# Other orders of the steps on each engine and other PSUM places in a pipelined decoder layer

## The reference

```python
x = _layernorm(x + linear_attention(x, Wq, bq, Wk, bk, Wv, bv, Wo, bo))
x = _layernorm(x + cross_attention(x, ctx, ctx))
x = _layernorm(x + ffn(x, w_gate, w_up, w_down))
```

## Time and profile before

| | |
|---|---|
| time, median of 3 runs | 1811.16 us (1810.85 to 1812.78) |
| the profiled execution | 1813.1 us |
| its span, first to last instruction | 1811.3 us |
| mean granted clock of TensorE | 0.964 of full speed |
| TensorE (PE) busy | 1626.2 us, 90% of the span |
| VectorE (DVE) busy | 1380.3 us, 76% |
| ScalarE (ACT) busy | 826.8 us, 46% |
| GpSimd (POOL) busy | 184.3 us, 10% |

### The profile page before, as it was taken

The page is one execution under the profiler, slowest core; times in us unless marked ns, Lnnn a source line. Parts: engine busy times, 40 slices in busy tenths (PEclk is TensorE's granted clock), DMA queues, the critical chain, the costliest instruction groups (busy, mean ns, idle before and its releaser), DMA issues.

```text
span 1811.3 us, 25396 instructions
## 1 busy us (share of the span) xinstructions
PE 1626.2 (90%) x10470; PEld 1002.6 (55%) x10470; DVE 1380.3 (76%) x1759; ACT 826.8 (46%) x784; POOL 184.3 (10%) x154
## 2 busy tenths in 40 slices
PE   7776599999999999999999999999999999996865
PEld 5443465656666555656656555656556655653533
DVE  3567887787968687787969697877869687876846
ACT  1124237264554536363554536363544536372633
POOL 0222301001010201011010202010010202010000
PEclk9887799999999999999999999999999999997979
DMA  5242220405050311304050401304050502204000
GB/s 204 50 111 97 48 18 30 51 7 74 1 80 1 67 13 39 41 18 63 1 79 1 75 6 50 30 25 56 2 79 1 79 1 57 24 19 47 7 7 12
DMA packets 100122, 75.73 MB, mean 42 GB/s; under 512 B 6044, under 2 KB 85148, under 8 KB 99496
## 3 DMA queue, kind: packets, MB, share of 16 engines
q1 hardware_dynamic: 100008, 74.10, 23.1%
HBM read 52.58 MB, written 20.97 MB: 41 GB/s over the span
## 4 chain that ended last, share of the span: by engine, by line
PE 78%; DVE 9%; ACT 8%; issue 2%; DMA 1%; POOL 1%; SPq 1%; POOLq 0%; ACTq 0%; DVEq 0%
PE psum L508 12%; PE psum L658 11%; PE psum L596 7%; PE psum L609 6%; PE psum L685 6%; PE psum L702 6%; PE psum L532 6%; PE psum L554 6%; PE psum L575 5%; ACT ffn_mem L733 3%; PE psum L638 2%; PE psum L694 2%; DVE ffn_mem L1086 2%; PE psum L677 1%; PE psum L542 1%
## 5 line engine op out<-in xcount | busy, mean ns | idle before, releaser
L733 ACT ACTIVATE ffn_mem<-psum 128x1024 f32<-128x1024 f32 x160 | 159.9, 1021 | 390.4 <-PE psum L630 148.7
L1013 DVE TENSOR_REDUCE mneg<-psum 128x4 f32<-128x1024 f32 x256 | 306.5, 1219 | 37.7 <-PE psum L575 34.4
L736 ACT ACTIVATE attn_mem<-psum 128x1024 f32<-128x1024 f32 x256 | 249.4, 1019 | 87.2 <-PE psum L609 85.0
L575 PE MATMUL psum<-kst,attn_mem 96*128 96x256 bf16 x1024 | 149.4, 277 | 25.2 <-DMA attn_mem<-q_dram 8.7
L609 PE MATMUL psum<-attn_mem,kst 98*128 98x512 bf16 x512 | 148.1, 391 | 21.2 <-ACT attn_mem L736 10.7
L1144 POOL TENSOR_TENSOR grstd<-gvare,neg_half 128x1 f32<-128x1 f32 x32 | 17.6, 551 | 1353.6 <-DVE gvare L912 1353.6
L1105 DVE TENSOR_TENSOR ffn_mem<-ffn_mem 128x1024 f32<-128x1024 f32 x128 | 150.8, 1219 | 1.2
L685 PE MATMUL psum<-had,ffn_mem 128*128 128x128 f32 x1024 | 127.2, 277 | 22.2 <-ACT ffn_mem L733 22.2
L596 PE MATMUL psum<-attn_mem,vpad 128*32 128x256 f32 x2048 | 138.1, 394 | 2.5 <-ACT attn_mem L736 2.5
L575 PEld LDWEIGHTS psum<-kst,attn_mem 96*128 96x128 bf16 x1024 | 96.1, 99 | 76.1 <-issue 20.7
L824 ACT ACTIVATE ffn_mem<-psum,sc 128x1024 f32<-128x1024 f32 x64 | 69.7, 1114 | 148.2 <-PE psum L658 148.0
(11 more groups left out here) (152 smaller groups left out, 2489.5 us busy)
## 6 DMA issues: line engine op xcount, KB each, us to landing
attn_mem<-q_dram SPq DMA_DIRECT2D x192, 128.0 KB, 7.7
q_dram<-work SPq DMA_DIRECT2D x48, 256.0 KB, 2.8
x_in<-in_x SPq DMA_DIRECT2D x16, 512.0 KB, 3.8
out<-r SPq DMA_DIRECT2D x32, 256.0 KB, 2.2
ffn_mem<-in_L_ffn_w_gate SPq DMA_DIRECT2D x1, 4096.0 KB, 21.6
ffn_mem<-in_L_ffn_w_up SPq DMA_DIRECT2D x1, 4096.0 KB, 16.0
ffn_mem<-in_L_ffn_w_down SPq DMA_DIRECT2D x1, 4096.0 KB, 13.8
c_in<-in_ctx SPq DMA_DIRECT2D x16, 128.0 KB, 2.2
```

The lines of the kernel that those rows point to most:

```text
L575: last = mm(region(f"max{u}")[:, i * T:(i + 1) * T], qst[0:KR, GQ * g + i, t * P:(t + 1) * P], kst[0:KR, g, :], start=True, stop=True)
L733: return nc.scalar.activation(dst, src, ACT.Copy)
L736: return nc.scalar.activation(dst, src, ACT.Exp, **kw)
L1013: nc.vector.tensor_reduce(mneg[:, h, t, GQ * g:GQ * (g + 1)], region(f"max{u}").rearrange("p (h t) -> p h t", h=GQ), AX_X, ALU.max, negate ...
```

## The change

The same steps stand on the same engines, with other places in the five lists, other batch offsets where a list now begins at another point of the cycle, and other PSUM slots. The functions behind the steps are unchanged. The whole diff:

```diff
--- before.py
+++ after.py
@@ -158,38 +158,38 @@
         tern = [qd[:, :], qdT[:, :, :].rearrange("p c t -> p (c t)")]
 
         orders = {
-            "sp": """t_load.2-3 t_load.0-2 x_fetch-1 x_split-2 x_stack.0-2 t_load.1-2 x_stack.1-2 s_mT.0-2 s_mT.1-2 c_store.0-3
-                c_store.1-3""",
-            "pe": """s_scores.9-3/1 s_pv.3-3/0 s_scores.10-3/3 t_quarter.1.1-3/0 s_scores.11-3/2 s_pv.4-3/1 s_scores.12-3/0
-                s_scores.13-3/3 s_pv.5-3/2 s_scores.14-3/1 t_quarter.1.2-3/3 t_quarter.1.3-3/2 s_scores.15-3/0 s_out.0-3/2
-                x_split-2/3 s_pv.6-3/1 s_pv.7-3/0 x_load-1/1 t_sum.2-3/1 s_out.1-3/2 x_k.0-1/0 x_q.0-1/1 t_quarter.2.0-3/3
-                t_quarter.2.1-3/3 t_quarter.2.2-3/3 t_quarter.2.3-3/2 x_k.1-1 d_hT-3/3 x_q.1-1 t_sum.0-2/2 d_hx-3/2 x_kst.0-2/3
-                x_q.2-1 s_max.0-2/0 s_max.1-2/2 s_max.2-2/3 x_q.3-1 d_qx-3/0 s_max.3-2/2 c_up.0-3/0 s_max.4-2/3 c_gate.0-3/2
-                c_gate.1-3/3 c_up.1-3/1 x_v.0-1/2 s_max.5-2/0 x_v.1-1 t_quarter.0.0-2/0 c_gate.2-3/3 c_gate.3-3/1
-                t_quarter.0.1-2/0 x_c-1/2 s_max.6-2/1 c_up.2-3/0 c_up.3-3/3 c_dT.0.0-3/0 s_max.7-2/3 c_dT.0.1-3/2 c_H.0.0-3/1
-                x_o.0-1/0 x_kst.1-2/1 c_H.0.1-3/3 s_mT.0-2/2 x_o.1-1 t_quarter.0.2-2/2 c_dT.1.0-3/3 c_dT.1.1-3/1 c_H.1.0-3/1
-                s_max.8-2/0 c_H.1.1-3/3 s_max.9-2/2 s_scores.0-2/1 s_max.10-2/0 s_scores.1-2/2 s_max.11-2/3 s_scores.2-2/1
-                c_q.0-3/3 s_pv.0-2/2 s_max.12-2/0 s_max.13-2/1 s_scores.3-2/3 c_dn.0-3/2 s_scores.4-2/1 s_pv.1-2/0
-                s_scores.5-2/3 s_max.14-2/2 c_q.1-3/1 t_sum.1-2/3 s_max.15-2/3 s_pv.2-2/0 s_scores.6-2/2 s_mT.1-2/3
-                s_scores.7-2/1 t_quarter.0.3-2/1 c_dn.1-3/0 t_quarter.1.0-2/3 s_scores.8-2/3""",
-            "act": """s_scores.11-3 s_scores.12-3 s_scores.13-3 s_scores.14-3 t_quarter.1.2-3 t_quarter.1.3-3 s_scores.15-3 x_split-2
-                x_load-1 t_quarter.2.0-3 t_quarter.2.1-3 x_q1-2 t_quarter.2.2-3 t_quarter.2.3-3 d_hT-3 x_k.1-1 d_hx-3 x_kst.0-2
-                d_round-3 d_qx-3 x_q.3-1 c_gate.0-3 c_gate.1-3 c_gate.2-3 c_gate.3-3 c_dT.0.0-3 c_H.0.0-3 t_quarter.0.0-2
-                c_dT.0.1-3 t_quarter.0.1-2 s_mT.0-2 t_quarter.0.2-2 c_H.0.1-3 x_kst.1-2 c_dT.1.0-3 c_dT.1.1-3 c_round.0-3
-                c_H.1.0-3 c_H.1.1-3 s_scores.0-2 s_scores.1-2 s_scores.2-2 c_q.0-3 c_round.1-3 s_scores.3-2 s_scores.4-2
-                s_scores.5-2 c_q.1-3 s_mT.1-2 s_scores.6-2 s_scores.7-2 t_quarter.0.3-2 t_quarter.1.0-2 s_scores.8-2
-                t_quarter.1.1-2 s_scores.9-2 s_scores.10-2""",
-            "dve": """t_quarter.1.0-3 t_lower.1.1-3 t_quarter.1.1-3 t_lower.1.3-3 s_pv.3-3 t_quarter.1.2-3 t_quarter.1.3-3 x_norm-2
-                s_pv.4-3 s_pv.5-3 s_out.0-3 s_pv.6-3 s_pv.7-3 x_split-2 t_abs.2-3 t_sum.2-3 s_out.1-3 t_lower.2.1-3
-                t_quarter.2.0-3 d_ln-3 t_quarter.2.1-3 t_lower.2.3-3 t_quarter.2.2-3 t_quarter.2.3-3 x_q2-2 d_norm-3 t_abs.0-2
-                d_had-3 x_k.1-1 t_sum.0-2 t_lower.0.1-2 d_hx-3 s_max.0-2 d_qx-3 s_max.1-2 s_max.2-2 s_max.3-2 t_quarter.0.0-2
-                s_max.4-2 x_q.3-1 t_quarter.0.1-2 c_up.0-3 c_up.1-3 c_fly.0.0-3 s_max.5-2 t_lower.0.3-2 c_fly.0.1-3 x_v.1-1
-                t_quarter.0.2-2 c_fly.0.2-3 t_quarter.0.3-2 c_fly.0.3-3 x_ctx-1 s_max.6-2 c_up.2-3 c_up.3-3 c_fly.1.0-3
-                c_fly.1.1-3 s_max.7-2 c_fly.1.2-3 c_fly.1.3-3 c_H.0.1-3 s_mT.0-2 x_o.1-1 c_qd.0-3 s_max.8-2 s_max.9-2 s_max.10-2
-                s_max.11-2 c_H.1.1-3 s_pv.0-2 s_max.12-2 s_max.13-2 t_abs.1-2 c_qd.1-3 c_dn.0-3 s_pv.1-2 t_sum.1-2 s_max.14-2
-                s_max.15-2 s_pv.2-2 c_norm.0-3 s_mT.1-2 c_dn.1-3 c_norm.1-3""",
-            "pool": """x_o.1-2 x_prep-2 t_lower.1.0-3 t_lower.1.2-3 t_lower.2.0-3 s_copy-2 t_lower.2.2-3 d_ln-3 c_dn.0-3 t_lower.0.0-2
-                c_dn.1-3 t_lower.0.2-2""",
+            "sp": """c_store.0-3 t_load.2-2 t_load.0-1 x_fetch x_split-1 x_stack.0-1 c_store.1-3 x_stack.1-1 s_mT.0-1 t_load.1-1
+                s_mT.1-1""",
+            "pe": """s_pv.7-3/1 x_load-1/0 s_out.1-3/2 t_sum.2-3/1 x_split-2/3 t_quarter.1.3-3/2 t_quarter.2.0-3/2 x_k.0-1/1
+                t_quarter.2.1-3/0 t_quarter.2.2-3/2 t_quarter.2.3-3/0 t_sum.0-2/0 x_k.1-1 x_kst.0-2/3 d_hT-3/0 d_hx-3/2
+                x_v.0-1/0 x_v.1-1 d_qx-3/1 s_max.0-2/2 s_max.1-2/3 t_quarter.0.0-2/1 s_max.2-2/0 c_gate.0-3/1 s_max.3-2/2
+                c_up.0-3/3 s_max.4-2/0 c_gate.1-3/2 s_max.5-2/3 s_max.6-2/1 c_up.1-3/0 t_quarter.0.1-2/0 s_max.7-2/2 x_q.0-1/3
+                c_gate.2-3/0 c_up.2-3/1 x_q.1-1 s_mT.0-2/2 c_gate.3-3/0 x_kst.1-2/1 x_q.2-1 x_q.3-1 s_max.8-2/1 c_up.3-3/2
+                c_dT.0.0-3/1 s_scores.0-2/0 x_c-1/2 s_scores.1-2/3 c_H.0.0-3/1 c_dT.0.1-3/0 s_max.9-2/2 c_H.0.1-3/3 s_max.10-2/1
+                s_scores.2-2/2 x_o.0-1/0 s_scores.3-2/2 x_o.1-1 s_max.11-2/2 c_dT.1.0-3/3 c_dT.1.1-3/1 s_max.12-2/0 s_pv.0-2/3
+                c_H.1.0-3/1 t_quarter.0.2-2/0 s_max.13-2/3 c_H.1.1-3/2 t_quarter.0.3-2/0 t_sum.1-2/1 s_scores.4-2/0 s_max.14-2/1
+                s_scores.5-2/2 s_max.15-2/3 c_q.0-3/0 s_scores.6-2/1 s_mT.1-2/2 s_pv.1-2/3 c_dn.0-3/0 s_scores.7-2/3 s_pv.2-2/2
+                c_q.1-3/1 s_pv.3-2/3 t_quarter.1.0-2/2 s_scores.8-2/0 t_quarter.1.1-2/3 s_scores.9-2/2 s_scores.10-2/3
+                c_dn.1-3/1 t_quarter.1.2-2/1 s_scores.11-2/3 s_pv.4-2/0 s_scores.12-2/1 s_scores.13-2/3 s_pv.5-2/2
+                s_scores.14-2/0 s_out.0-2/1 s_scores.15-2/2 s_pv.6-2/3""",
+            "act": """s_scores.0-2 s_scores.1-2 c_dT.0.1-3 c_H.0.0-3 c_H.0.1-3 s_scores.2-2 s_scores.3-2 c_dT.1.0-3 t_quarter.0.2-2
+                c_dT.1.1-3 t_quarter.0.3-2 c_round.0-3 c_H.1.0-3 c_H.1.1-3 s_scores.4-2 s_scores.5-2 c_q.0-3 s_mT.1-2
+                s_scores.6-2 c_round.1-3 s_scores.7-2 c_q.1-3 s_scores.8-2 t_quarter.1.0-2 t_quarter.1.1-2 s_scores.9-2
+                s_scores.10-2 s_scores.11-2 t_quarter.1.2-2 s_scores.12-2 s_scores.13-2 s_scores.14-2 s_scores.15-2 x_load
+                t_quarter.1.3-2 x_split-1 t_quarter.2.0-2 t_quarter.2.1-2 t_quarter.2.2-2 t_quarter.2.3-2 x_q1-1 d_hT-2 x_k.1
+                x_kst.0-1 t_quarter.0.0-1 d_hx-2 d_round-2 d_qx-2 c_gate.0-2 t_quarter.0.1-1 c_gate.1-2 c_gate.2-2 c_gate.3-2
+                s_mT.0-1 x_kst.1-1 x_q.3 c_dT.0.0-2""",
+            "dve": """s_pv.6-3 s_pv.7-3 t_abs.2-3 t_sum.2-3 x_norm-2 s_out.1-3 t_lower.2.1-3 t_quarter.2.0-3 t_quarter.2.1-3
+                t_lower.2.3-3 d_ln-3 t_quarter.2.2-3 t_abs.0-2 t_quarter.2.3-3 x_split-2 t_sum.0-2 d_norm-3 d_had-3 x_q2-2
+                t_lower.0.1-2 t_quarter.0.0-2 d_hx-3 t_quarter.0.1-2 d_qx-3 x_k.1-1 x_v.1-1 s_max.0-2 s_max.1-2 s_max.2-2
+                s_max.3-2 c_up.0-3 s_max.4-2 s_max.5-2 s_max.6-2 c_up.1-3 c_fly.0.0-3 s_max.7-2 c_fly.0.1-3 t_quarter.0.2-2
+                c_up.2-3 c_fly.0.2-3 t_lower.0.3-2 s_mT.0-2 c_fly.0.3-3 t_quarter.0.3-2 s_max.8-2 c_up.3-3 x_q.3-1 c_fly.1.0-3
+                x_ctx-1 c_fly.1.1-3 s_max.9-2 c_fly.1.2-3 s_max.10-2 c_fly.1.3-3 c_H.0.1-3 x_o.1-1 s_pv.0-2 s_max.11-2 c_qd.0-3
+                s_max.12-2 t_abs.1-2 t_sum.1-2 s_max.13-2 s_max.14-2 s_max.15-2 c_H.1.1-3 s_mT.1-2 s_pv.1-2 c_qd.1-3 c_dn.0-3
+                t_quarter.1.0-2 s_pv.2-2 s_pv.3-2 t_lower.1.1-2 c_norm.0-3 t_quarter.1.1-2 t_lower.1.3-2 c_dn.1-3
+                t_quarter.1.2-2 t_quarter.1.3-2 s_pv.4-2 s_pv.5-2 s_out.0-2 c_norm.1-3""",
+            "pool": """t_lower.0.0-3 t_lower.0.2-3 x_o.1-2 t_lower.1.0-3 t_lower.1.2-3 t_lower.2.0-3 t_lower.2.2-3 x_prep-2 d_ln-3
+                s_copy-2 c_dn.0-3 c_dn.1-3""",
         }
 
         def parsed(entry):
```

## The result

The changed kernel takes 1794.81 us (median of 4 runs, 1793.91 to 1796.03) against 1811.97 for the kernel before in the same runs: ratio 0.9906, 95% interval 0.9894 to 0.9919. It is faster, by 0.9%, but the forecast was 1770 and the range ended at 1791. The profiled execution has a span of 1792.6 us, 18.7 less than before, where the steps of the prediction add up to 41.5.

What follows compares the result with a forecast made beforehand. TensorE and short waits bound the cycles, weights passing through one buffer the opening. Opening 215.1, thirteen cycles 1296, drains 101 and 95.5, tail 62.1 sum to 1769.7 against 1811.3; 41.5 off the median gives 1770 us, range 1755 to 1791.

Steps and rivals of the forecast that it cites:

- Step (a): Opening: with t_abs.0 and the quarters earlier, the last gate quarter ends and the up load leaves at 102.4 us.
- Step (b): Opening: q blocks ahead of the up load end s_max.8's 8.72 us wait; up scale at 133.3 instead of 147.5, -14.2.
- the rival on the opening: Opening does not shorten: GpSimd's t_lower holds t_quarter, or DMA contention moves loads; 1779 (half lost) or 1788; chance 0.10.
- q blocks in time: Full cycle: q blocks in place at 24.1, s_max.0 reached at 24.3; the rival that they come late had 0.06.
- (c): Opening, up scale to down load: 20 us instead of 21.5; the load leaves at 153.3, down scale at 176.5, -19.
- (d): Opening, down scale to the first batch's d_had: 24.6 us instead of 25.4, so d_had at 201.1.
- (e): Opening, d_had to d_qx: 14.0 us instead of 12.8; d_qx of batch 0 at 215.1, -18.5.
- The wait sum of 4.4: Full cycle: TensorE's waits in the new order, 0.72 at d_hT, 1.28 at d_hx and 2.44 others, against 5.8 before.
- the base of 95.3: Full cycle: TensorE's 82 steps without any wait add up to 95.3 us, below which no order can go.
- The 0.72 us at d_hT: Full cycle: TensorE reaches d_hT at 11.95 and waits 0.72 us, as d_had ends only at 12.7.
- the s_copy term: Full cycle: s_copy on GpSimd now runs beside d_norm on VectorE; 0.37 us added, bounds 0 and 0.85.
- the waits come back: Rival: thin margins and unlisted short waits keep the cycle at 101.1 us, time 1788; chance 0.20.

Runs made afterwards that it cites:

- experiments 3 and 4: The up load's place in SyncE's queue alone: put back between the q blocks in the changed kernel, 1816.89 us; moved behind them in the kernel before, 1804.14 us.
- experiment 3: The changed kernel with the up load (t_load.1) back ahead of the second half's q blocks on SyncE: 1816.89 us, ratio 1.0033 to the kernel before.
- Experiment 1: The changed kernel with all twelve t_lower on VectorE, none on GpSimd: 1782.82 us, ratio 0.984 to the kernel before.
- Experiment 9: The changed kernel with s_copy back ahead of d_ln on GpSimd: 1795.79 us, ratio 0.9914 to the kernel before.

## Why the prediction was wrong, point by point

**Right.** The direction. Step (a): the up load left at 102.47, forecast 102.4. Step (b): t_abs.1 at 123.28 and the up scale at 132.90, forecast 124 and 133.3; experiments 3 and 4 show that it was the load's place in the queue, and experiment 3 that it is worth 25 us in the new order, since without it the 4 MB load delays the blocks for which TensorE then stands still. The down load landed in 13.9 us, forecast 13.8, so DMA contention, the other half of the rival on the opening, did not come; t_abs.2 followed 14.06 us after the load's issue (157.92 to 171.98). In the cycle the waits at d_hx and c_H.0.1, the end of the one at c_H.1.0, and q blocks in time; both drain cycles within 0.8.

**Wrong: steps (c) and (d) of the opening.** The step that failed is the premise "every matmul, copy and DMA keeps its price and the sum is only over waits". VectorE's steps did not keep theirs: t_lower went from 1.28 to 4.03 us in (c), and in (d) x_norm from 0.99 to 6.12 and t_lower to 6.28. "The same steps in the new order take 20" measured 25.0 (132.90 to 157.92), and "in the new order 24.6" measured 30.9 (181.60 to 212.49): 11.3 of the 12.1 us, the rest is (e) with 0.7. Experiment 1 measures the same two stretches with GpSimd out of the way: 23.4 and 23.15. So in (d) GpSimd's work is the whole miss, the hold and the 1.69 us for the root behind it. In (c) taking it away gave back 1.6 of the 5.0, net of the two t_lower (2.6 us) that VectorE then computes itself. By the rows the held t_lower is 2.8 of the 5.0 (4.03 less 1.28); the rest are waits of VectorE for TensorE and ScalarE ahead of the quarters (1.18, 1.08, 0.77, 1.12 us in its rows between s_mT.0 and s_pv) that the 20 did not hold in full.

This was the rival "t_quarter on VectorE is held by t_lower on GpSimd", which I gave a tenth, but for the step: VectorE's t_lower and x_norm were held most, hardly t_quarter (at most 2773 ns, median 2345). The argument against it was that t_lower already ran beside t_quarter before. The view that would have warned of it was there, lines 717 and 959 (t_quarter) of the kernel before, and I had read starts and not spreads:

```profile
L717 DVE TENSOR_SCALAR act_f<-ffn_mem,wnthr x6: 1271/1286/2340, 83.3 to 211.1; 128x2048 bf16<-128x2048 f32 x6
...
L959 DVE SCALAR_TENSOR_TENSOR qdT<-ffn_mem,wthr,act_f x6: 2337/2345/5683, 94.5 to 214.6; 128x2048 bf16<-128x2048 f32 x6
```

Maxima of 2340 and 5683 beside medians of 1286 and 2345 are two held steps, 4.4 us, in the old order. VectorE's timeline of the kernel before has three more beside GpSimd's t_lower; here with the one of 5.68:

```profile
94.48 3.85 DVE L959 SCALAR_TENSOR_TENSOR qdT<-ffn_mem,wthr,act_f 128x2048 bf16<-128x2048 f32 x1
...
157.07 5.68 DVE L959 SCALAR_TENSOR_TENSOR qdT<-ffn_mem,wthr,act_f 128x2048 bf16<-128x2048 f32 x1
...
198.35 1.83 DVE L1036 TENSOR_TENSOR r<-att,y 128x512 f32<-128x512 f32 x1
...
206.28 4.18 DVE L912 TENSOR_SCALAR fvare<-fmv 128x2 f32<-128x2 f32 x1
```

Against 2.35, 0.69 and 0.17 us elsewhere that makes some 9 us of held time in the old order, my estimate (the step after the last one starts 2.2 us late), so the 21.5 and 25.4 us that I started from in (c) and (d) had most of it in them. In the new order it is some 16 us (x_q2 2.9, x_norm 5.1, t_lower 0.5, 2.8 and 5.0), and more of it lies on the chain: without GpSimd's t_lower the same opening is 13.4 us shorter, in the old order 2.0.

The page that I had weighed for s_copy was the one for this: the Trainium skill, "SBUF — State Buffer", section "Who interferes with whom", says that tensor_scalar on VectorE can run in modes that take the port pair which VectorE shares with GpSimd, that a VectorE instruction with two inputs in SBUF contends with GpSimd's reads, that one with at most one such input outside those modes does not, and that who comes second waits for the whole instruction. The trace of the opening agrees for t_lower and for the x_norm of 181.92, and x_q2, with its two SBUF inputs, takes 4.08 us beside GpSimd's first t_lower where it takes 1.22 in a cycle:

```profile
71.50 4.08 DVE L1008 TENSOR_TENSOR work<-work 128x1024 bf16<-128x1024 f32 x1 [0.81 <-ACT work L733]
```

For d_norm beside s_copy, both tensor_scalar, the price of a whole block did not come, and whether there is a block is open. VectorE's timeline, d_norm in the cycle shown:

```profile
813.85 1.06 DVE L1046 TENSOR_SCALAR y<-r,fmv,frstd 128x512 f32<-128x512 f32 x2
```

s_copy runs from 813.58 to 814.64, and they cost each other 0.06 and 0.2 us. But d_norm's pair ends 0.27 us after s_copy, here and within 0.02 us in the other cycles, as the held pair of x_norm ended 0.28 us after GpSimd's t_lower (188.04 and 187.76): the second of its two steps may have been held too, when little of s_copy was left. Nor does every such pair show a whole block: the x_norm of the earlier trace rows ended at 813.56, and the GpSimd step beside it, begun ahead of it, ran from 811.99 to 814.23. I took the 0.37 us of that pair for s_copy and did not ask the rule about t_lower.

**Wrong in size: the cycle.** Forecast 99.7, measured 100.38. The wait sum of 4.4 became 5.04, added up as in the prediction from TensorE's rows, and the base of 95.3 held. The 0.72 us at d_hT never came: VectorE reached d_had sooner, because GpSimd's root took 0.72 us beside x_split and not 1.63 as beside x_q2. GpSimd's timelines, before:

```profile
824.81 1.63 POOL L1144 TENSOR_TENSOR frstd<-fvare,neg_half 128x2 f32<-128x2 f32 x1 [4.06 <-DVE fvare L912]
```

and after:

```profile
812.88 0.72 POOL L1144 TENSOR_TENSOR frstd<-fvare,neg_half 128x2 f32<-128x2 f32 x1 [4.01 <-DVE fvare L912]
813.58 1.06 POOL L1141 TENSOR_SCALAR vpad<-c_in 128x256 f32<-128x256 f32 x1
```

x_split reads PSUM and one SBUF tile, x_q2 two SBUF tiles; that this is the reason fits the page's rule and was not tried alone. Experiment 9 puts the s_copy term at 0.06 instead of 0.37. Against the 0.72 that did not come stand 1.36 (5.04 less 3.68) that I did not have, most of it some ten pauses of 0.06 to 0.11 us from one step to the next that no list of waits shows. A cycle of before has 2.1 us of waits beyond TensorE's idle time (5.8 less 3.69), one of after 2.2 (5.04 less 2.82): in both orders about the same, and my list for the new one held only a part of it. This is the rival "the waits come back", by half.

**The tail** was 1.1 us longer with a granted clock of 0.85 where before had 0.91; the cause was not looked for.

## What to carry to other kernels

Ahead of a reorder, read the spread of each step's duration (minimum, median, maximum) and not only its median: a maximum far above it can be a step that stood still beside another engine, and in an order that takes the slack out of a stage such a hold costs more. The same edit was worth 2.0 us in the loose order and 13.4 in the tight one, the place of one load in a queue 9.4 and 25. For a wait that is to be covered, follow all that hangs on the moved step, the readers of its PSUM place too, to the next wait; a long cover only moved it.
